# The last layer cut into pieces, its four batches overlapped and begun inside the last feed-forward item of the layer before

## The reference: what is computed

```python
# layer 3, attention: h = layernorm(x)
Q = h @ Wq + bq;  K = ctx @ Wk + bk;  V = ctx @ Wv + bv
x = x + softmax(Q @ K.T / sqrt(128)) @ V
# layer 3, feed-forward: h = layernorm(x)
scores = softmax(h @ W_gate)                    # 7 columns
w = top_k(scores, 2), divided by its sum
x = x + h @ W_shared.T + (w, where within capacity) * (h @ W_expert.T) + bias
```

## Time and profile before

| | us |
|---|---|
| median of 3 runs | 1012.13 |
| the runs | 1011.17 to 1013.39 |
| the profiled execution's own time | 1012.16 |
| its span, first to last instruction | 1010.4 |
| PE busy in the span | 912.1 (90%) |
| DVE busy | 581.9 |
| ACT busy | 432.4 |
| POOL busy | 283.9 |

### The profile page before, as it was taken

The page is one execution under the profiler, slowest core; times in us unless marked ns, Lnnn a source line. Parts: engine busy times, 40 slices in busy tenths (PEclk is TensorE's granted clock), DMA queues, the critical chain, the costliest instruction groups (busy, mean ns, idle before and its releaser), DMA issues. The chain is left out here.

```text
span 1010.4 us, 15438 instructions
## 1 busy us (share of the span) xinstructions
PE 912.1 (90%) x5522; PEld 648.1 (64%) x5522; DVE 581.9 (58%) x1403; ACT 432.4 (43%) x795; POOL 283.9 (28%) x404
## 2 busy tenths in 40 slices
PE   2689999999999898999989799998999999999776
PEld 2555446465555444888877545545888878888665
DVE  3665757675757574455556367674536454354477
ACT  1345555667654555233332356655223232222330
POOL 7411514545644532010211055332001010010243
PEclk9989989999979799999999889999999999999995
DMA  6000000000010210000000211100000000000001
GB/s 153 4 2 14 1 15 2 15 2 18 19 53 2 76 36 9 14 1 1 1 1 1 77 29 37 44 24 13 2 1 1 1 1 1 1 1 1 1 1 42
DMA packets 27573, 18.10 MB, mean 18 GB/s; under 512 B 6221, under 2 KB 25770, under 8 KB 27370
## 3 DMA queue, kind: packets, MB, share of 16 engines
q1 hardware_dynamic: 27498, 17.12, 6.1%
HBM read 15.63 MB, written 1.05 MB: 17 GB/s over the span
## 5 line engine op out<-in xcount | busy, mean ns | idle before, releaser
L1327 DVE TENSOR_REDUCE mneg<-PS 128x2 f32<-128x308 f32 (+1 forms) x384 | 180.4, 515 | 115.5 <-PE PS L880 114.7
L1490 DVE TENSOR_TENSOR work<-PS,work 128x512 f32<-128x512 f32 (+2 forms) x168 | 114.8, 685 | 169.3 <-PE PS L1065 126.1
L1796 ACT ACTIVATE work<-PS 128x512 f32<-128x512 f32 (+2 forms) x168 | 99.8, 596 | 245.9 <-PE PS L1065 232.1
L1773 ACT ACTIVATE work<-PS 124x512 f32<-124x512 f32 (+1 forms) x272 | 156.8, 601 | 92.8 <-PE PS L1000 91.9
L1079 PEld LDWEIGHTS PS<-down_w,work 128*128 128x128 f32 (+2 forms) x1344 | 157.8, 191 | 5.7 <-DVE work L1490 1.3
L1079 PE MATMUL PS<-down_w,work 128*128 128x128 f32 (+2 forms) x1344 | 158.3, 275 | 1.0 <-DVE work L1490 1.0
L1063 PE MATMUL PS<-xh_sb,arena 128*128 128x512 f32 (+2 forms) x336 | 138.0, 411 | 9.6 <-DVE work L1490 9.6
L1065 PE MATMUL PS<-xh_sb,arena 128*128 128x512 f32 (+2 forms) x336 | 132.6, 395 | 0.0
L1064 PE MATMUL PS<-xl_sb,arena 128*128 128x512 f32 (+2 forms) x336 | 132.0, 393 | 0.0
L1867 POOL TENSOR_SCALAR rstd<-bn_mv 128x4 f32<-128x4 f32 x32 | 7.3, 227 | 436.2 <-DVE bn_mv L1225 436.1
L880 PEld LDWEIGHTS PS<-kb_sb,qxt_sb 97*128 97x128 f32 x256 | 45.4, 197 | 63.5 <-issue 33.8
(11 more groups left out here) (183 smaller groups left out, 1277.4 us busy)
## 6 DMA issues: line engine op xcount, KB each, us to landing
ctx_rep<-in_ctxT SPq DMA_DIRECT2D x12, 308.0 KB, 3.2
stage<-in_w SPq DMA_DIRECT2D x8, 256.0 KB, 4.2
stage<-in_wg SPq DMA_DIRECT2D x8, 176.0 KB, 2.4
stage<-in_wu SPq DMA_DIRECT2D x8, 176.0 KB, 2.4
x_res<-in_x SPq DMA_DIRECT2D x4, 256.0 KB, 3.9
down_w<-in_w SPq DMA_DIRECT2D x1, 1024.0 KB
down_w<-in_wd SPq DMA_DIRECT2D x8, 128.0 KB
out<-x_res SPq DMA_DIRECT2D x4, 256.0 KB, 2.3
```

What stands on the lines that cost most here:

```text
L1327: dve.tensor_reduce(mneg[:, a % 2, t, h0:h0 + 2], PS[:, bank_of["mx", a, m], 0:2 * (KT0 if layer == 0 else KC)].rearrange("p (h n) -> p h ...
L1490: dve.tensor_tensor(HH[0:rows, e % 2, j, :], PS[0:rows, 2 * (n % 2) + 1, :], SS[0:rows, n % 2, :], ALU.mult).then_inc(*sig["h"].mark((i, n)))
L1773: act.activation(p_tile(i, n)[0:rows, :], PS[0:rows, n % 2, :], ACT.Exp, scale=SCALE).then_inc(*sig["p"].mark((i, n)))
L1796: act.activation(SS[0:rows, n % 2, :], PS[0:rows, bank, :], ACT.Silu).then_inc(*sig["act"].mark((i, n)))
```

## The change

The A3 and F3 items no longer stand in the list of items that every engine runs over. All their steps have become pieces (`a3t`, `a3o`, `f3` are new names), and a table, `LAST_SLOTS`, places the 14 steps of each batch among the slots of the last F2 item (its slots 0 to 25 are the tiles; the rest are new slots behind it, up to 60). From slot 30 on a piece may take any of the eight PSUM banks. Each batch has its own buffers for the normalised `x` and its transpose, and there are two of Q, K, V, the probabilities and their transpose, all in tiles that no one needs by then (`qx_sb`, `q_sb`, `hidden`, `ctx_rep`, ...). The arithmetic stays.

```diff
-MAIN = [i for i, item in enumerate(ITEMS) if item[0] != "F0"]
+MAIN = [i for i, item in enumerate(ITEMS) if item[0] not in ("F0", "A3", "F3")]
...
+LAST_NORMS = [j for b in range(B) for j in (6 * B + b, 7 * B + b)]
 def ring(j):
-    return NORMS.index(j) % 2
+    return 2 + ITEMS[j][2] if j in LAST_NORMS else NORMS.index(j) % 2
...
+    if kind == "F2":
+        if b == B - 1:
+            for b0 in range(B):
+                last_layer(put, b0, LAST_SLOTS[b0])
...
+LAST_SLOTS = (
+    (4, 4, 25, 30, 32, 34, 37, 38, 39, 42, 44, 45, 46, 47),
...
+    (30, 29, 37, 42, 45, 47, 49, 52, 53, 56, 57, 58, 59, 60),
+)
+def last_layer(put, b, at):
+    i, j = 6 * B + b, 7 * B + b
+    for t in range(T):
+        put(at[0], "ln", i, t)
+    put(at[1], "norm", i)
+    for x, name in zip(at[2:7], ("xt", "proj3", "scores3", "a3t", "a3o")):
+        put(x, name, i)
+    for t in range(T):
+        put(at[7], "ln", j, t)
+    put(at[8], "norm", j)
+    put(at[9], "xt", j)
+    for n in range(3):
+        put(at[10 + n], "late", j, n)
+    put(at[13], "f3", j)
...
-        QT3, KT3 = work[:, 0:512], work[:, 512:512 + KC]
+        QT3 = (HH0[:, 1, :], HH0[:, 2, :])
+        KT3 = (HH0[:, 3, 0:KC], HH0[:, 3, 256:256 + KC])
...
-                if i == 6 * B - 3:
+                if i == 5 * B:
                     sp.wait_ge(*sig["resid"].at(5 * B - 1))
                     load(WF3[:, 0:D], A["we3T"], "w_ffn3_in", 0)
...
-                    elif kind == "A3":
-                        attention3_step(i, n)
-                    elif n == 0:
-                        ffn3(i)
+                    if i == 6 * B - 1 and n >= n_slots(i) + 4:
+                        i_main = None
+                    else:
+                        i_main = i
                     for p in now:
-                        piece(i, p)
+                        piece(i_main, p)
```

254 lines of the change are left out of this document (130 added, 124 removed), and 2 rows, old and new, of the table LAST_SLOTS.

## The result

The changed kernel takes 1004.26 us (median of 10 runs, 1000.15 to 1008.08), the kernel before 1012.41 beside it on the same chip (median of 10, 1008.70 to 1016.38). The ratio is 0.992, interval 0.989 to 0.994: faster by 8.2 us, where 1005.1 was forecast.

A forecast was written before the change was run, and what follows sets the result against it. No engine fills the last layer: a chain through ScalarE, TensorE and VectorE bounds its attention, VectorE its feed-forward part. Last add at 976.5 + 9.2 + 8.8 + 5.4 = 999.9, rounded up to 1000.6: gain 7.0, 1005.1 us (1003.9 to 1006.7).

The forecast's parts named there:

- The start: F2 items of batches 2 and 3: moving early statistics gains 0.85 us; their new slots cost nothing.
- Into the attention: Ahead of the first exponentials: batch 1's transposes add 0.45 us, batch 3's statistics 0.55.
- The attention laps: First to last exponentials: 8.4 + 1.8 for a clock fall + 8.0 + 8.6 = 26.8 us.
- a second such stretch: Rival, longer time at half clock: two more stretches cost 1.8 us each, 1008.7 us; chance 16 of 100.
- The feed-forward part: Last exponentials to last add: VectorE is the thread; batches take 3.0, 9.2, 8.8 and 5.4 us; the gain is here.
- 1.8 us of holds: Batch 2's feed-forward lap: VectorE held up by GpSimd for 1.8 us, within a lap of 8.8.
- with its PE work under it: Batch 3's feed-forward lap: 5.35 us of VectorE steps, TensorE's work hidden beneath, as before.
- Held up by GpSimd: F3 norms beside VectorE's router steps: two-input SBUF steps and GpSimd exclude each other; 2.5 us in the sum.
- The clock in the feed-forward part: TensorE kept at 0.50 there; an early return would save about 0.4 us, as only the last batch waits.
- half clock through all laps: Rival in the attention: TensorE's links double in every lap, 12.4 us for 1.8, 1015.7 us; slower, chance 6 of 100.
- GpSimd's holds at their worst: Rival in the feed-forward part: three norms fall on router steps, +7 us, 1012, no change; chance 5 of 100.
- A better overlap: Rival in the last layer: waits of 0.8 and 0.55 and 2.5 of holds go, 999.5 us; chance 6 of 100.

The follow-up runs named there:

- e2_stats_back: Changed kernel with statistics and norms of batches 0 and 1 back in slots 0 to 3 of the last two F2 items; 1003.48 us.
- e4_fill_order: Changed kernel with one table entry changed: batch 1's projections in slot 33, ahead of batch 0's probability transposes; first lap 10.47 us.
- e3_filler: Changed kernel plus ten identity matmuls on TensorE in the wait behind batch 0's scores; first lap 8.25 us, second 10.34.
- e11_dve_load: Changed kernel plus one unused VectorE copy behind the gates of each F3 item; last exponentials to last add 27.74 us.
- e12_table: Changed kernel with a new table: next batch's scores ahead of this batch's product with V, F3 pieces closer; feed-forward part 32.73 us.
- e8_after_again: The changed kernel unaltered, run again beside other runs; 1002.25 us.
- e5_three_moves: Changed kernel with batch 1's projections, batch 3's A3 statistics and batch 3's F3 statistics moved in the table; 1005.61 us.
- e6_no_idle: Kernel of e5_three_moves plus unread identity matmuls where TensorE waits, in the attention and ahead of F3's transposes; 1005.99 us.
- e10_best: Kernel of e12_table with the last two GpSimd passes of F3's normalization replaced by ScalarE activations; feed-forward part 32.7 us.
- e1_old_order: Changed kernel's buffers, banks and early statistics, but last layer's steps in the order of the kernel before; 1011.8 us, ratio 0.998.

## Why the prediction was right, point by point

**The start.** Right. Both waits of 0.44 are gone, and the item between the two starts is 0.9 shorter than with the statistics back and 0.4 shorter than before. From the first start to the last down products 1.2 us were gained, for 0.85 forecast. The three sets of statistics at slots 4, 8 and 12 cost nothing to be seen, and TensorE shows no wait behind them up to the last down products.

**Into the attention.** Forecast +1.0 us ahead of the first exponentials, less the wait of 0.44 in that item: +0.56. Measured from the item's start: 948.75 - 885.96 = 62.79, before 946.53 - 884.14 = 62.39 (884.14 is where that start came): +0.40. Right. Moving the statistics of batch 3 back behind the maxima gave 0.39 of the 0.55 that I had put to them.

**The attention laps.** Forecast 26.8 with one fall of the clock for 1.8. Measured 28.17 in the first profile, 26.59 in the second. The working of a lap at full clock was right to 0.15: 8.25, 8.07 and 8.5 measured (the last from the runs e2_stats_back, 8.51, and e4_fill_order, 8.49), for 8.4, 8.0 and 8.6. One fall in the first lap costs 1.7 (9.93 - 8.25), for 1.8; in the second it cost 0.7 in the first profile (8.78 - 8.07) and 2.3 in e3_filler (10.34 - 8.07). What I had not reckoned with is that the falls wander: none of the runs of this order without fillers in every wait was free of one, the first profile has two. The forecast had one fall in the first lap, and a second such stretch as a rival with 16 of 100; in the first profile that rival's event came about in part (one such stretch more, not two), and in the other there was one fall, as forecast, but in the third lap and not in the first. I had also not counted GpSimd's hold of the maxima's scaling, 1.1 us in the third lap of the first profile and nothing in the second.

**The feed-forward part.** Forecast 26.4, measured 26.55 and 25.64. The forecast's thread is right for all but the end: VectorE bounds the laps of batches 1 and 2, as e11_dve_load shows. (VectorE was not "busy without a break" in the last 25 us, as the signs had it: 22.24 of 26.55.) Inside, two terms were off and cancelled, which is luck. For batch 2 I had put 1.8 us of holds; only 0.7 fell there (L1411 at 992.71, 0.46 for 0.19, and L1417 at 993.63, 0.65 for 0.19), and the lap was 7.54 for 8.8. For batch 3 I had 5.35, "with its PE work under it"; but its statistics stand behind the adds of batch 1, and the chain from them to its router ran past VectorE's other work. VectorE waited 1.57 us and the lap was 7.03. The two errors, -1.3 and +1.6, leave the sum as it was.

What the part gained over before, 9.8 us, has two main sources. VectorE is busy for 30.86 us there before and for 22.24 after: 8.6 less. By each step's length over its shortest in these runs, 5.2 us of before's 30.86 were time held by GpSimd, and 1.5 of the 22.24. The other 1.2 us are shorter waits. Of the 8.6, 4.9 are work that has moved under the attention laps, which is the forecast's reason, and 3.7 are holds that do not fall here. The forecast had holds in its sum, 2.5 us, 1.0 too many; it did not say that less time held than before is a good part of the gain.

**Held up by GpSimd.** The rule that the Trainium skill gives ("SBUF — State Buffer", "Who interferes with whom": two operations of VectorE and GpSimd at the shared port pair exclude each other) agrees with these traces in kind. It hits more than the two-input steps that I had counted: L1593 has one input in SBUF and 4 columns, and took 1.29 us beside a bias add that began in the same instant:

```profile
975.59 1.27 POOL L1932 TENSOR_TENSOR x_res<-x_res,b_out 128x512 f32<-128x512 f32 x1
```

The amount varies by execution and by table. From the first exponentials to the last add it is 5.8 us in the kernel before, 2.6 and 2.2 in the two profiles of the changed one, and 6.8 in e12_table.

**The clock in the feed-forward part.** I kept 0.50 on the row of before, and it was 0.50 for about half of that part (0.74 in the mean). I also wrote that only the last batch waits for TensorE, and put about 0.4 us to it at the other clock. The last batch does wait, and it is worth more. VectorE at the last router in the first profile of the changed kernel and then in e8_after_again, where TensorE ran that router at full clock (1.06 us, for 1.87):

```profile
998.01 0.19 DVE L1391 COPY lg_sb<-PS 128x28 f32<-128x28 f32 x1 [1.57 <-PE PS L936]
```

```profile
993.50 0.19 DVE L1391 COPY lg_sb<-PS 128x28 f32<-128x28 f32 x1 [0.40 <-PE PS L936]
```

The last laps are 7.03 and 5.72. So in this order the lower clock costs about 1.3 us at the end, by this one pair of profiles. With the statistics of batch 3 moved ahead (e5_three_moves, e6_no_idle) it costs nothing, and in e10_best's order 4.8.

**The sum.** 7.0 us forecast. Measured 8.2 in the medians, 6.4 in the profiled pair from a common mark, 7.6 from the group of down products with the second profile (70.19 - 62.56) and 5.1 with the first. The time lies 0.8 us under the forecast and inside its own range; that it came so near is partly luck, since the two errors of the feed-forward part cancelled and the totals scatter by more. That scatter I had too small: 0.2% from three runs of before, where ten show 0.8% (1008.70 to 1016.38). What failed of the rivals: half clock through all laps, and GpSimd's holds at their worst, came in none of the executions of this kernel that were profiled. A better overlap, which I had given 6 of 100, is not in this kernel; but its lap was no bound of the work, as opening the ring shows.

**What stays open.** What brings the clock down at one place and not at another. In the second lap, stays of 0.76 and 1.11 were followed by a fall in e3_filler and by none in e8_after_again, at the same products. And why GpSimd's operations fall on fewer of VectorE's steps in e1_old_order than in before, whether for the buffers and banks or for when the part began.

## What to carry to other kernels

When batches are laid over each other, look for the ring that is left: a lap that is longer than the work of its busiest engine is a chain, and one move in the order (the next batch's scores ahead of this batch's product) can open it. What that frees is then bound by the next engine, so find in the trace which one it will be, and at which clock, before you count the gain. Compare executions by marks inside the trace when the totals scatter by more than the effect.

## What the runs showed of the hardware that was not expected

- The granted clock went to 0.50 after stays of TensorE of about 0.8 to 4 us, at other places in the two profiled executions of the changed kernel. Among the attention laps it came back after 3 to 7 us; in the feed-forward part of the first profile it stayed down from 989 to 1002, with TensorE busy for 11.15 of those 13 us (990 to 992: 2.00 of 2.00 us at 0.50). With fillers in most of its stays it held up to 998.
- The load of ScalarE's table (1.28 us) is hidden while ScalarE waits for the operand of the first exponential. A 0.20 us activation of another function placed ahead of that exponential exposes it.
- The position of the last layer in the span, behind all but the same instructions, ranged from 933.27 to 941.99 us over the profiled executions of these kernels, as measured at the group of down products. So much of the scatter of the totals arises ahead of the part that was changed. The one pair of profiles of the same kernel (the changed one) differs by 2.2 us ahead of that mark and by 2.5 behind it.
- Time in which GpSimd's operations hold VectorE's steps makes up 5.2 us of the feed-forward part in the kernel before (36.4 us) and 2.4 in e1_old_order (32.7 us), with the same 105 instructions in it. So it can be gained or lost by a change that was made for another reason.
